# A selective-scan pipeline: the second half of each u*B product also waits for VectorE's product with C, with new instruction orders

## The reference

```
A_disc = jnp.exp(delta[..., None] * A)                       # 256 channels, 16 states
B_x = delta[..., None] * Bm[:, :, None, :] * x1[..., None]   # u*B, with u = delta * x1
def step(hc, inp):
    a, b = inp
    hc = a * hc + b
    return (hc, hc)
_, hs = jax.lax.scan(step, h0, (Ad_t, Bx_t))
y = jnp.einsum('btdn,btn->btd', hs, Cm)
```

## Time and profile before

| | |
|---|---|
| median of 3 runs | 855.99 us |
| lowest and highest | 852.4 and 860.42 us |
| the profiled execution's own time | 855.11 us |
| its span, first to last instruction | 853.3 us |
| TensorE's mean granted clock | 0.89 of full speed |
| busy: PE, DVE, ACT, POOL | 81%, 72%, 48%, 46% |

### The profile page before, as it was taken

How to read it: one execution, slowest core, us unless ns; L and a number is a source line. 1 busy time by engine, 2 the same in 40 slices (tenths; PEclk the granted TensorE clock), 3 DMA queues, 4 the chain that set the end, 5 groups by cost and what they waited for, 6 DMA issues and landing times. The chain is left out here.

```text
span 853.3 us, 12511 instructions
## 1 busy us (share of the span) xinstructions
PE 689.6 (81%) x4232; PEld 409.9 (48%) x4232; DVE 611.0 (72%) x1063; ACT 410.0 (48%) x816; POOL 391.6 (46%) x473
## 2 busy tenths in 40 slices
PE   5478756897889878998789778987898789976678
PEld 2345524444645555445544555455544564444225
DVE  1963376787869786977788787878697769854582
ACT  1323431771558354843477256825484337532532
POOL 6631232483339423844457234942394127411561
PEclk7577966999899999898989898998989898988798
DMA  5221300350044203430135004410343004100410
GB/s 133 86 97 37 116 22 23 127 166 27 2 153 128 89 0 84 144 138 0 48 136 178 7 1 151 151 59 1 102 145 117 2 16 154 46 2 6 146 53 7
DMA packets 40457, 66.10 MB, mean 77 GB/s; under 512 B 7282, under 2 KB 29635, under 8 KB 38083
## 3 DMA queue, kind: packets, MB, share of 16 engines
q1 hardware_dynamic: 38242, 64.57, 23.1%
q10 hardware_dynamic: 2176, 1.05, 0.4%
HBM read 57.68 MB, written 7.86 MB: 77 GB/s over the span
## 5 line engine op out<-in xcount | busy, mean ns | idle before, releaser
L765 POOL TENSOR_TENSOR shared<-u,bcrow 128x512 f32<-128x512 f32 x128 | 205.9, 1638 | 93.3 <-DVE u L1148 70.6
L1159 DVE TENSOR_TENSOR_SCAN shared<-ps_f,shared 128x512 f32<-128x512 f32 x128 | 150.9, 1209 | 26.0 <-PE ps_y L1198 9.9
L1198 PE MATMUL ps_s<-stack_mem 72*128 72x128 bf16 (+3 forms) x1024 | 148.4, 266 | 18.9 <-DVE mx L1062 12.6
L1062 DVE TENSOR_REDUCE mx<-ps_s 128x2 f32<-128x512 f32 (+1 forms) x192 | 127.1, 686 | 41.8 <-PE ps_s L1198 38.6
L1198 PE MATMUL ps_y<-shared,ident 128*128 128x512 f32 x256 | 124.0, 616 | 18.6 <-DVE shared L1164 18.5
L1198 PEld LDWEIGHTS ps_s<-stack_mem 74*128 74x128 bf16 (+1 forms) x1024 | 87.0, 106 | 83.7 <-DVE mx L1062 26.6
L926 ACT ACTIVATE ps_f<-delta,amat 128x255 f32<-128x255 f32 x256 | 110.6, 478 | 31.5 <-DVE shared L1159 17.9
L857 ACT ACTIVATE probs<-ps_s 128x512 f32<-128x512 f32 x192 | 106.5, 597 | 34.9 <-PE ps_s L1198 34.4
L1164 DVE TENSOR_TENSOR shared<-shared,bcrow 128x1024 f32<-128x1024 f32 x64 | 89.7, 1401 | 2.2
L1198 PE MATMUL ps_y<-zero_bf 128*128 128x512 bf16 x293 | 88.2, 416 | 1.4 <-DVE zero_bf L999 1.0
L728 POOL TENSOR_TENSOR rstd<-mv,cst 128x2 f32<-128x2 f32 x32 | 6.2, 195 | 175.0 <-DVE mv L979 175.0
(11 more groups left out here) (212 smaller groups left out, 1022.2 us busy)
## 6 DMA issues: line engine op xcount, KB each, us to landing
bcrow<-bc_dram SPq DMA_DIRECT2D x64, 512.0 KB, 4.0
stack_mem<-stack_dram SPq DMA_DIRECT2D x96, 192.0 KB
stack_dram<-parts SPq DMA_DIRECT2D x24, 256.0 KB, 2.3
x_tm<-in_L_attn_x_dram ACTq DMA_DIRECT2D x8, 128.0 KB, 2.2
xb<-in_L_attn_x_dram SPq DMA_DIRECT2D x8, 128.0 KB, 2.2
out_dram<-y_out SPq DMA_DIRECT2D x8, 128.0 KB, 2.0
fmem<-in_L_attn_conv_w_dram SPq DMA_DIRECT2D x1, 512.0 KB
lmem<-in_L_ffn_W_dram SPq DMA_DIRECT2D x2, 256.0 KB
```

The lines of the kernel that those rows point to most:

```text
L765: G.tensor_tensor(bx[:, j % 2, c], u[:, c].unsqueeze(1).to_broadcast([P, 2, T]), bcrow[:, j % RING, 0], ALU.mult).then_inc(bx_sb, 1)
L1062: V.tensor_reduce(mx[:, a, min(i, 1), hd[0]:hd[-1] + 1:2], ps_s[:, n % 2].rearrange("p (h n) -> p h n", h=len(hd)), AX.X, ALU.max).then_in ...
L1159: V.tensor_tensor_scan(hs[:, j % HB, c].rearrange("p n t -> p (n t)"), ps_f[:, c, :], bx[:, j % 2, c].rearrange("p n t -> p (n t)"), 0.0, ...
L1198: return nc.tensor.matmul(o, lhsT, rhs, start=start, stop=stop, **kw)
```

## The change

One wait is added to `products` on GpSimd. For j of 2 and more, P(j,1) waits for H(j-2):

```diff
                         if j >= 2 or not is_first(b):
                             pool.wait_ge(hs_sb, b * 16 + 2 * j + c - 3)
+                        if j >= 2 and c == 1:
+                            pool.wait_ge(hc_dve, b * 8 + j - 1)
                         G.tensor_tensor(bx[:, j % 2, c], u[:, c].unsqueeze(1).to_broadcast([P, 2, T]),
```

Since two lines are added, a line of TensorE or ScalarE at 765 or below stands two lines lower in the new kernel (1198 becomes 1200, 857 becomes 859). The tables of the order are changed too, some 25 lines, of which two matter most (both in `PLAN`):

```diff
-        "norm": [12.1],
+        "norm": [9.7],
...
-        "scan": [68, 71.6, 75.6, 86.2, 89.7, 97.5, 102.5, 106.4],
+        "scan": [68, 71.6, 75.6, 84.7, 89.7, 97.5, 102.5, 106.4],
```

More of the change, by code:

```diff
@@ L44 @@
         "core": [48.9, 55.2, 55.3, 73.9, 76],
-        "rows": [68.7, 71.2, 71.5, 71.8, 72.1, 82.9, 87.2, 90.1, 93.8],
+        "rows": [68.7, 71.2, 71.5, 71.8, 72.1, 77.7, 77.8, 80.6, 93.8],
     },
@@ L48 @@
         "core": [-2, 43],
-        "prep": [15.5, 28.9, 40.6, 43.9],
+        "prep": [15.6, 28.9, 40.6, 44],
         "lora_ffn": [31.2, 41.9],
@@ L64 @@
         "mamba": [47.1, 47.2, 62.2, 63.8],
-        "scan": [67.4, 69, 71.4, 75.5, 78, 79.3, 81.7, 82.9, 85.7, 86.5, 89, 92.1, 94.5, 94.6, 97.3, 98.5],
+        "scan": [67.4, 69, 71.4, 75.5, 78, 79.3, 81.7, 82.9, 85.7, 86.5, 89, 92.1, 94.8, 94.9, 97.7, 98.8],
     },
@@ L99 @@
             "prep": [14.4, 14.4, 17.9, 20.2, 37.9, 45.9],
-            "core": [17.5, 19.5, 19.9, 29.4, 31.5],
+            "core": [17, 19, 19.4, 28.9, 31],
         },
@@ L104 @@
             "core": [0.5, 28.6],
-            "prep": [6.2, 15, 21.5, 24.9],
+            "prep": [6.2, 15.8, 22.3, 25.8],
         },
@@ L108 @@
             "setup": [1.1, 1.9, 9.1],
-            "prep": [0.7, 4, 8.3, 9.8, 11.4, 12.5, 15.5, 22.4, 26.5],
+            "prep": [0.7, 2.7, 7, 8.6, 10.2, 12.5, 15.5, 22.4, 26.5],
             "core": [4.4, 38.9, 39.5, 40.4, 41, 41.6, 43.7, 44.2, 44.7, 45.6, 46.2, 46.7, 47.6, 48.1, 48.7, 48.8,
@@ L116 @@
                      39.6, 41.5, 42.3, 43, 43.6, 44.6, 45.4, 46.1, 47, 48.8],
-            "prep": [25.3, 27.2],
+            "prep": [25.8, 27.8],
             "norm_std": [68.5],
@@ L120 @@
         "pe": {
-            "prep": [0, 8.3, 14, 16, 18, 19.3, 31],
-            "setup": [0.8, 6.6, 9.8],
+            "prep": [0, 8.3, 14, 16, 17.8, 17.9, 31],
+            "setup": [0.2, 6.6, 9.8],
             "core": [18.9, 19.8, 20.7, 22, 22.9, 24.1, 24.8, 25.7, 28.1, 28.7, 29.6, 30.2, 31.5, 31.6, 32.4, 33.6,
@@ L146 @@
         "act": {
-            "core": [0, 62, 62.5, 64.5, 65, 65.5, 66.5, 67, 68.3, 69.6, 70.1, 70.7, 72.9, 73.4, 74, 76.6, 77.1, 77.6,
-                     78.2, 80.2, 80.7, 81.3, 83.8, 84.3, 84.9, 85.8, 88.4],
+            "core": [0, 62, 62.5, 64.5, 65, 65.5, 66.5, 67, 68.3, 69.6, 72.8, 73.3, 75.6, 76.1, 76.7, 79.2, 79.7,
+                     80.2, 80.8, 82.9, 83.4, 83.9, 86.6, 87, 87.6, 88.4, 91.1],
             "prep": [0.8, 2.3, 3.8, 6.4, 7.9, 9, 15.5, 21.7, 25.9],
@@ L152 @@
             "mamba": [47.6, 53.2, 57.3, 59],
-            "scan": [63, 63.8, 67.5, 68.8, 71.2, 72.2, 74.6, 75.8, 78.7, 79.4, 81.9, 83.1, 86.5, 87.7, 90.1, 90.5],
+            "scan": [63, 63.8, 67.5, 68.8, 71.2, 72.2, 74.6, 77.3, 78.7, 79.4, 81.9, 83.1, 86.5, 87.7, 90.1, 90.5],
         },
@@ L200 @@
         "dve": {
-            "mamba_out": [1, 7.9, 9.4],
-            "norm": [3.1, 6.2, 8],
+            "mamba_out": [1, 7.5, 9.4],
+            "norm": [3.1, 6.2, 7.9],
             "ffn": [8.7, 11.1, 11.6, 13.2, 14, 21.9, 24.7, 25.6, 26.7, 28.5, 36.6, 38.3],
             "lora_ffn": [17.3, 20.7, 30.4, 32.1],
-            "mamba": [41.5, 51.2, 60.9],
+            "mamba": [43, 51.2, 60.9],
             "scan": [64.8, 66, 67.3, 68.4, 69.6, 70.9, 72, 73.2, 74.5, 75.7, 76.8, 78.1, 79.3, 80.5, 81.8, 82.9,
@@ L212 @@
             "lora_ffn": [11.7, 14.6, 18.6, 24.1, 27.3, 27.4],
-            "ffn": [15.4, 18.1, 20.7, 20.8, 29.8, 33.5],
-            "mamba": [33.6, 33.7, 42.6, 42.7],
+            "ffn": [15.4, 18.1, 20.7, 20.8, 29.8, 30.4],
+            "mamba": [30.5, 33.2, 42.6, 42.7],
             "scan": [67.7, 71.3, 75, 78.6, 82.3, 85.9, 89.5, 93.2],
@@ L236 @@
             "mamba_out": [0.9],
-            "lora_ffn": [5.6, 7.7, 7.8, 7.9, 8, 8.1],
+            "lora_ffn": [9.4, 11.4, 11.5, 11.6, 11.7, 11.8],
             "warm_late": [1.5, 2.7, 3.9, 5.1, 7.5, 8.7, 9.6, 9.7, 12.3, 13.5, 14.7, 15.8, 19.3, 20.5, 21.7, 22.9],
```

2 lines of the change are left out of this document (1 added, 1 removed).

## The result

The changed kernel takes 860.3 us (median of 20 runs, 851.8 to 864.6), the kernel before 853.0 (20 runs, 848.8 to 860.7). The ratio is 1.0053, with an interval of 1.0030 to 1.0077: 4.5 us slower, between 2.6 and 6.6. That is clear of the noise, and still within the 1% that the prediction counts as no change. The two medians lie 7.3 us apart, more than the interval allows; the text goes by the ratio, and the longest run of the change, in a slow state of the chip (864.6 us), is not in it. The prediction was 861.0 in a range of 854.0 to 866.5. The profiled execution after has a span of 855.4 us, only 2.1 over the one before; it won 3.9 us ahead of the first scan, which starts at 158.85 instead of 162.78.

What follows compares the result with a forecast made beforehand. No engine is full: a turn is one chain through several engines, with VectorE in fixed order. 855.1 + 0 + 3.7 + 5.0 - 1.2 - 1.5 = 861.1, given as 861.0 us, range 854 to 866.5.

Steps and rivals of the forecast that it cites:

- The new wait: Middle scans: GpSimd's second half product waits for the product with C of two steps back; counted 0 us.
- Early sum and late factors: Turns 1 to 6: exponential of piece 23 ahead of the factors starts step 6's scan 0.6 us later; +3.7 us.
- combT ahead of xT: Heads of turns 1 to 5: wout, behind the line product needing xT, comes 0.99 us late; +5.0 us in all.
- ScalarE in turn 0: First scan: earlier decay factors start step 4 about 2.3 us earlier, 0.7 to 1.7 left at scan end; -1.2 us.
- The tail: Tail: six more zero matmuls in TensorE's gaps save 3 us or nothing; the middle taken, -1.5 us.
- falls a little later: Tail case: TensorE's clock still falls, only a little later, and nothing is saved.
- stays up: Tail case: TensorE's clock does not fall, saving 3 us in all.
- The rest: Linesn transposes, setup swaps and the last turn's moved zero matmuls: counted 0, with 0.5 us either way.
- The early sum pays: Rival, middle scans: the 9.9 us of waits for TensorE's sum of step 3 go; 847.5 us, chance 0.06.
- The heads are absorbed: Rival, turn heads: a wait behind z ends by something unmoved, so 856 us, no change seen; chance 0.16.
- The third: Rival: the new wait binds, 3 us, and TensorE's clock falls more often at turn heads; 865 to 867, chance 0.18.

Runs made afterwards that it cites:

- mended: Changed kernel with TensorE's wout put ahead of the first line product in turns 1 to 5; ratio 1.0006 to the kernel before, +0.5 us.

## Why the prediction was right, point by point

- **The new wait** (counted 0): right. Alone +0.9 us with an interval on both sides of 0; P(j,1) at 1.27, H at 1.38, and a step of the change takes 3.67 us (H at 444.48, the next at 448.15), as worked out. In the scans of the change in which P(j,0) is second it does not bind: in batch 6 throughout, in batch 1 up to step 6. That is why the mean of P is 1.48 and not the 1.40 of the forecast. By the exclusive lock of the Trainium skill (SBUF — State Buffer, "Who interferes with whom") the second of two stands still until the first is done; the trace agrees for the product on GpSimd (2.25 us, and 2.31 where it meets H at its start). For H it agrees only in part: with 0.30 us of the half product left it takes 1.38 us, 0.15 more than alone and not 0.30.
- **Early sum and late factors** (+3.7): the mechanism was right, the size not. The wait ahead of S(6,0) is now put down to ScalarE. From the start of the scan, S(6,0) came at 25.74 us before and at 26.12 after: +0.38 instead of +0.6. The term of the sum that was off is the lateness of piece 22: it was taken to be 1.03 us late and was 0.74 (22.78 against 22.04 us from the scan's start), since the sum started right behind piece 21 and held TensorE for 1.72 us until piece 22 began, not 1.87. And the count of six full turns was too much: alone the two moves cost +1.3 us (-0.7 to +3.2), and in the profile with these two alone what the scan loses was regained in the next turn's head, for a reason that stays open.
- **combT ahead of xT** (+5.0): right in place and size. z's wait grew by 0.99 us in each of five turns, alone +5.3, mended -4.0.
- **ScalarE in turn 0** (-1.2, "0.7 to 1.7"): right that S(4,0)'s 2.27 us go and that P(6,0)'s row takes most of it back, but more is taken back: the scan is shorter by 0.8 to 0.9 us in three profiles and by 0.2 in four, as that row lands earlier or later.
- **The tail** (-1.5, between 0 and -3): right as a pair of cases. In seven profiles with the new tail four have it 0.8 us shorter, as if the clock "falls a little later", and three 3.1 us, as if it "stays up". The mean is -1.8.
- **The rest** (0): not settled. These parts with turn 0 and the tail gave -4.2 us with an interval that reaches from -6.7 to -1.6; the setup on average 0.5 us earlier, less than its spread.
- **The rivals.** The early sum pays: no, exponential 23 starts at 461.18, not before 459.5. The heads are absorbed: no. The third, that the clock falls more often, was not seen: the mean granted clock of the change's runs is 0.893, that of the kernel before in the later comparisons 0.893 to 0.897. But it pointed at what matters most here: I read the slow stretches, and priced only the tail's.

Added up the parts measured alone give 0.9 + 1.3 + 5.3 - 4.2 = +3.3 us, the change itself +4.5, and both intervals hold the other. The mechanism of the largest term was right, and the forecast of +5.0 from 856.0 to 861.0 is near the measured +4.5. That it is so near, and that the median of 860.3 falls 0.7 us from 861.0, is partly luck: the early sum was counted 2.4 us too high and the gains 1.5 us too low, against parts known to 2 or 3 us each, and the kernel before itself has a median of 853.0 over 20 runs, not 856.0.

## What to carry to other kernels

When two copies on one engine change places, look at the order of their consumers on the next engine: wout stood behind a product that needed the other copy, and a swap that made its own input ready earlier made it a microsecond later. Where two operations shut each other out, as H and P(j,1) do here, it won nothing to let one of them wait at a semaphore instead of in the engine; a short duration in the profile after is no gain. And where an execution has the same stage at two lengths, look at the granted clock at the stage's head before changing anything in the stage.

## What the runs showed of the hardware

- TensorE's clock fell from 1.00 to 0.50 at the head of batch 3's scan, where TensorE had been idle for 0.87 us shortly ahead of the fall and was idle for 0.83 us shortly behind it. It then stayed there for 6.8 us, with TensorE busy for most of them, and the scan took 2 us longer. With two pairs of zero matmuls of 0.59 us in these gaps it was at 1.00 in 18 of 18 scans of three kernels.
- Whether a scan's head was slow differed from scan to scan in one execution, and with it the place and length of the slow stretch in the next turn's head (3.4 to 13.7 us). Where scans had become 0.5 us longer (early sum and exponential 23 alone) the next head's stretch was 3.4 us instead of 6.8. Whether such moves make up a part of this kernel's spread of some 10 us from run to run, and of what the parts measured alone seem to gain or lose, was not tested.
- H takes longer too when it starts while a half product is nearly done, but by less than what is left of it: 1.28 us with 0.2 us left, 1.38 with 0.3 us left, 1.23 with nothing in its way.
